# A 16-head attention layer's start is re-ordered: parts of q and k made per half from PSUM, all q/k projections before the row maxima, value projections between them, gates computed during the input load

## The reference

```python
x = x + _L0_attn_a_ref(_layernorm(x), Wq, bq, Wk, bk, Wv, bv, Wo, bo, gates...)   # layer "aa"
x = x + _L0_ffn_ref(...); x = x + _L0_attn_b_ref(...); x = x + _L0_ffn_ref(...)
x = x + _L1_attn_a_ref(_layernorm(x), Wqkv, Wproj, bproj)                         # layer "ac"
x = x + _L1_ffn_ref(...); x = x + _L1_attn_b_ref(...); x = x + _L1_ffn_ref(...)
...
q, k, v = (proj(Wq, bq), proj(Wk, bk), proj(Wv, bv))
scores = jnp.einsum('bhqd,bhkd->bhqk', q, k) / math.sqrt(hd)
order_bonus = jax.nn.sigmoid(order_gate) * (position_bias * 0.05)
justice_adjustment = jax.nn.sigmoid(justice_gate) * ((mean_score - scores) * 0.1)
attn = jax.nn.softmax(scores + order_bonus + justice_adjustment + ..., axis=-1)
out = jnp.einsum('bhqk,bhkd->bhqd', attn, v)
return out @ Wo.T + bo
```

## Time and profile before

| what | value |
|---|---|
| median of 3 runs | 1435.81 us (1435.34 to 1439.43) |
| profiled execution, span from the first to the last instruction | 1435.6 us |
| TensorE matmul busy | 1349.0 us (94%) |
| VectorE busy | 895.4 us (62%) |
| ScalarE busy | 694.1 us (48%) |
| GpSimd busy | 278.4 us (19%) |
| input load | 0 to 14.6 us |
| layer aa, before the first row maximum / the 14 slots | 14.6 to 37.9 us / 37.9 to 58.7 us |
| layer ac, before the first row maximum / the 14 slots | 626.5 to 641.9 us / 641.9 to 662.6 us |

### The profile page before, as it was taken

The page is one execution under the profiler, slowest core; times in us unless marked ns, Lnnn a source line. Parts: engine busy times, 40 slices in busy tenths (PEclk is TensorE's granted clock), DMA queues, the critical chain, the costliest instruction groups (busy, mean ns, idle before and its releaser), DMA issues. The chain is left out here.

```text
span 1435.6 us, 32894 instructions
## 1 busy us (share of the span) xinstructions
PE 1349.0 (94%) x13699; PEld 738.4 (51%) x13707; DVE 895.4 (62%) x2147; ACT 694.1 (48%) x1037; POOL 278.4 (19%) x343
## 2 busy tenths in 40 slices
PE   7999998999679988999999989999899999989999
PEld 3355555474345774563555554436355555555436
DVE  3899994666486456749999826433655555535431
ACT  5487776646483325535777752111444444442110
POOL 4322513001230000043000000110533433210110
PEclk9999999999879999999999999999999999999999
DMA  3323300100300000022222030000300000000000
GB/s 87 70 38 65 65 14 1 34 1 2 118 0 4 17 1 16 0 45 42 43 39 36 3 117 0 1 0 7 64 13 17 15 13 14 9 1 1 1 0 29
DMA packets 33957, 37.47 MB, mean 26 GB/s; under 512 B 9153, under 2 KB 24626, under 8 KB 33810
## 3 DMA queue, kind: packets, MB, share of 16 engines
q1 hardware_dynamic: 33810, 35.39, 11.2%
HBM read 18.43 MB, written 1.07 MB: 14 GB/s over the span
## 5 line engine op out<-in xcount | busy, mean ns | idle before, releaser
L616 DVE TENSOR_REDUCE row_max_pieces<-psum 128x1 f32<-128x512 f32 (+3 forms) x672 | 406.9, 647 | 112.4 <-PE psum L510 109.7
L717 ACT ACTIVATE probs<-psum 128x1024 f32<-128x1024 f32 (+7 forms) x384 | 343.7, 900 | 212.6 <-PE psum L510 212.2
L564 PE MATMUL psum<-probs,v_ones 128*32 128x256 f32 (+1 forms) x2688 | 238.8, 376 | 9.0 <-POOL probs L499 4.6
L510 PE MATMUL psum<-q_all,k_head 97*32 97x512 f32 (+3 forms) x1536 | 190.7, 487 | 0.0
L510 PE MATMUL psum<-k_stack,q_stack 96*32 96x512 bf16 x2048 | 158.8, 379 | 3.5 <-DMA k_stack<-arena 1.3
L510 PE MATMUL psum<-q_stack,k_stack 97*32 97x512 bf16 x2048 | 157.8, 379 | 0.0
L564 PEld LDWEIGHTS psum<-probs,v_ones 128*32 128x32 f32 x2688 | 88.0, 109 | 85.1 <-POOL probs L499 21.6
L510 PE MATMUL psum<-k_head_bf,q_all_bf 80*32 80x512 bf16 (+3 forms) x768 | 93.0, 328 | 2.3 <-ACT k_head_bf L2487 1.1
L510 PEld LDWEIGHTS psum<-q_all,k_head 97*32 97x32 f32 x1536 | 78.8, 109 | 29.5 <-issue 3.9
L510 PEld LDWEIGHTS psum<-k_stack,q_stack 96*32 96x32 bf16 x2048 | 56.5, 95 | 72.1 <-DVE row_max_pieces L616 20.4
L510 PEld LDWEIGHTS psum<-q_stack,k_stack 97*32 97x32 bf16 x2048 | 58.3, 96 | 49.4 <-ACT probs L717 3.7
(11 more groups left out here) (368 smaller groups left out, 2085.6 us busy)
## 6 DMA issues: line engine op xcount, KB each, us to landing
q_stack<-arena SPq DMA_DIRECT2D x32, 96.0 KB, 2.7
k_stack<-arena SPq DMA_DIRECT2D x32, 96.0 KB, 2.6
arena<-gd_g_sums SPq DMA_DIRECT2D x6, 512.0 KB, 6.1
q_stack<-arena SPq DMA_DIRECT2D x32, 64.0 KB, 2.3
k_stack<-arena SPq DMA_DIRECT2D x32, 64.0 KB, 2.3
x_tokens<-in_x SPq DMA_DIRECT2D x4, 256.0 KB, 3.6
k_stack<-arena SPq DMA_DIRECT2D x32, 32.0 KB, 2.3
q_stack<-arena SPq DMA_DIRECT2D x32, 32.0 KB, 2.0
```

The lines of the kernel that those rows point to most:

```text
L510: last = pe.matmul(o[j:j + 32], by[:, j:j + 32], rows, **flags)
L564: last = pe.matmul(psum[32 * g:32 * g + VW, PVB, a - g * D:D], V[:, c, h, :], pr[:, n % PB, a:(g + 1) * D], start=(c == 0), stop=(c == (2 ...
L616: last = dve.reduce_max(mx[:, h % 2, qt, i:i + 1], o[:, 0:plain], AX.X)
L717: act.activation(pr[:, n % PB, q_from(c):], psum[:, 2 * (n % 2):2 * (n % 2) + 2, :].rearrange("p a n -> p (a n)")[:, q_from(c):], ACT.Exp, ...
```

## The change

- The gates, the positions and the biases of q, k and v come in three DMAs that ScalarE issues at the start of `load_inputs`. ScalarE and VectorE compute gates, key factor and score scale before their part of the norm there; the sigmoid is made from an exponential, an addition and a reciprocal. A square root of a constant follows on ScalarE, before the first one of the norm. At the end of the load VectorE scales Wq by the score scale.
- All 16 projection matmuls of q and k come first, the second features' into banks 4 to 7. The first three pieces of the ring wait until ScalarE has taken these (`pe_ring`).
- Of the first features each half (512 tokens) is a unit of its own: ScalarE makes the high part straight from PSUM (L886), VectorE the rest from PSUM, bias and high part in one operation (L935), ScalarE the middle (L890), VectorE the low part (L938). The second features go over `qk_full` as before.
- The 16 value matmuls (now without the bias matmul) stand in slots 0 to 12: two each in slots 1, 3 and 5, one each in the others; they write banks 0 to 3. The copies of the values stand among the parts of the second features on ScalarE. The filler matmuls are gone. Before the first key scores TensorE waits for all eight copies.
- v's bias is added in `project_out`, when the attended features are copied (`Copy` becomes `Identity` with a bias).

```diff
 def load_inputs(nc, core, x_dram, loads, gates, wq, wq_loaded):
...
             def _(dve):
+                gates.dve(dve)
                 for t in range(NT):
                     dve.wait_ge(x_loaded[t // 2], 16)
                     norm.dve(dve, t)
+                gates.scale_queries(dve, wq, wq_loaded)
...
             def _(act):
+                gates.loads(act)
+                gates.act(act)
                 act.wait_ge(made, 4)
+                act.activation(spare[:], core.eps[:], ACT.Sqrt)
                 norm.act(act)
...
+    def act(self, act):
+
+        act.wait_ge(self.loaded, 48)
+        act.activation(self.g[:], self.g[:], ACT.Exp, scale=-1.0).then_inc(self.squashed, 1)
+        act.wait_ge(self.steps, 3)
+        act.activation(self.factor[:], self.factor[:], ACT.Exp).then_inc(self.exp_done, 1)
+
+    def dve(self, dve):
+
+        g, esc = self.g, self.score_scale
+        dve.wait_ge(self.squashed, 1)
+        dve.tensor_scalar(g[:], g[:], 1.0, None, ALU.add).then_inc(self.steps, 1)
+        dve.wait_ge(self.steps, 1)
+        dve.reciprocal(g[:], g[:]).then_inc(self.steps, 1)
+        dve.wait_ge(self.steps, 2)
+        dve.tensor_scalar(self.factor[:], self.pos, g[:, 1:2], 0.05, ALU.mult, ALU.mult).then_inc(self.steps, 1)
+        dve.tensor_scalar(esc[:], g[:, 0:1], -0.1 / HD ** 0.5, 1.0 / HD ** 0.5, ALU.mult, ALU.add).then_inc(self.steps, 1)
+        dve.wait_ge(self.steps, 4)
+        dve.tensor_scalar(self.bqk[:, 0, :], self.bqk[:, 0, :], esc[:, 0:1], None, ALU.mult)
...
+            V_BETWEEN = {m: (1, 2)[m in (1, 3, 5)] for m in range(13)}
+            V_UP_TO = {m: sum(V_BETWEEN[i] for i in range(m)) for m in range(14)}
...
                 def pe(pe):
                     pe.wait_ge(first_loaded, 32)
+                    for n in range(4):
+                        u = ORDER[n]
+                        for half in range(NH2):
+                            for k in range(KT):
+                                last = pe.matmul(Prep.bank(n, half), (wq, wk)[u // 2][:, k, (u % 2) * P:(u % 2 + 1) * P],
+                                                 XNT[:, k, cols(half)], start=(k == 0), stop=(k == KT - 1))
+                            last.then_inc(qk_ready, 1)
+                    pe.wait_ge(loaded, 48)
+
+                @staticmethod
+                def pe_ring(pe, n):
+                    pe.wait_ge(full_done, n + 1)
+
+                @staticmethod
+                def pe_between(pe, m):
+                    if m == 0:
+                        pe.wait_ge(r1, FIRST)
+                    for i in range(V_UP_TO.get(m, 0), V_UP_TO.get(m + 1, 0)):
+                        t, k = i // KT, i % KT
+                        last = pe.matmul(psum[:, t // 2, (t % 2) * D:(t % 2 + 1) * D], XNT[:, k, t * P:(t + 1) * P],
+                                         wv[:, k, :], start=(k == 0), stop=(k == KT - 1))
...
+                    def high_of(n, half):
+                        act.wait_ge(qk_ready, NH2 * n + half + 1)
+                        act.activation(parts[:, ORDER[n], 0, cols(half)], Prep.bank(n, half), **copied(n)).then_inc(hi, 1)
+
+                    def middle_of(n, half):
+                        act.wait_ge(r1, NH2 * n + half + 1)
+                        act.activation(parts[:, ORDER[n], 1, cols(half)], rest[:, n, cols(half)], ACT.Copy).then_inc(mid, 1)
...
                     for n in range(2):
                         for half in range(NH2):
-                            keep_full(n, half)
-                        high(n)
-                    middle(0)
-                    middle(1)
-                    for t in range(NT):
-                        keep_v(t)
+                            high_of(n, half)
+                            middle_of(n, half)
                     for n in range(2, 4):
                         for half in range(NH2):
                             keep_full(n, half)
+                    for n in range(2, 4):
                         high(n)
+                        for t in range(2 * (n - 2), 2 * (n - 1)):
+                            keep_v(t)
                         middle(n)
+                    for t in range(4, NT):
+                        keep_v(t)
...
                 def dve(dve):
+                            dve.wait_ge(hi, j + 1)
...
+                            dve.scalar_tensor_tensor(rest[:, n, cols(half)], Prep.bank(n, half), by,
+                                                     parts[:, ORDER[n], 0, cols(half)], op, ALU.subtract).then_inc(r1, 1)
+                            dve.wait_ge(mid, j + 1)
+                            dve.tensor_tensor(parts[:, ORDER[n], 2, cols(half)], rest[:, n, cols(half)],
+                                              parts[:, ORDER[n], 1, cols(half)], ALU.subtract).then_inc(lo, 1)
```

More of the change, by code:

```diff
@@ L158, in pe_behind, with load_inputs @@
             self.keep_busy(pe, 0, 1)
-def load_inputs(nc, core, x_dram, loads):
+def load_inputs(nc, core, x_dram, loads, gates, wq, wq_loaded):
     X, ident = core.X, core.ident
@@ L167, in load_inputs @@
         norm = Norm(core, "in", tmp)
+        spare = core.sb("spare_root", [P, 1], F32, tmp)
         with nc.Block() as block:
@@ new lines, in attention16 @@
+            cols = lambda half: slice(half * HALF, (half + 1) * HALF)
+            parts_done = lambda n: NH2 * (n + 1) if n < 2 else FIRST + n - 1
+            scale_of = lambda n: HD ** -0.5 if gates is None and ORDER[n] // 2 == 0 else 1.0
+            bias_of = lambda n: gates.bqk[:, ORDER[n] // 2, ORDER[n] % 2:ORDER[n] % 2 + 1]
+            V_BETWEEN = {m: (1, 2)[m in (1, 3, 5)] for m in range(13)}
+            V_UP_TO = {m: sum(V_BETWEEN[i] for i in range(m)) for m in range(14)}
+            def loads(sp):
@@ L812, in pe @@
                     pe.wait_ge(loaded, 48)
-                    if gates is not None:
-                        pe.wait_ge(gates_loaded, 80)
-                    for t in range(NT):
-                        o = psum[:, 4 + t // 2, (t % 2) * D:(t % 2 + 1) * D]
-                        for k in range(KT):
-                            last = pe.matmul(o, XNT[:, k, t * P:(t + 1) * P], wv[:, k, :],
-                                             start=(k == 0), stop=(k == KT - 1 and gates is None))
-                        if gates is not None:
-                            last = pe.matmul(o, core.ones[:], bv[:], start=False, stop=True)
-                        last.then_inc(v_ready, 1)
@@ L845, in keep_full @@
-                        scale = HD ** -0.5 if gates is None else esc[:]
-                        act.activation(full[:, n % 2, half * HALF:(half + 1) * HALF],
-                                       psum[:, 2 * (n % 2) + half, :], ACT.Identity,
-                                       bias=bqk[:, which, f:f + 1] if gates is not None else 0.0,
-                                       scale=1.0 if which else scale).then_inc(full_done, 1)
+                        act.activation(full[:, n % 2, cols(half)], Prep.bank(n, half), **copied(n)).then_inc(full_done, 1)
@@ L983, in attention16, with project_out @@
                             exp_kw={}, shift_dt=BF16, head_loads=Stacks, prep=Prep, aside=aside)
-        project_out(nc, core, tag, O, wo, next_loads)
-def project_out(nc, core, tag, O, wo, next_loads, tiles=KT, OT=None, xn=None):
+        project_out(nc, core, tag, O, wo, next_loads, bias=gates.bv if gates else None)
+def project_out(nc, core, tag, O, wo, next_loads, tiles=KT, OT=None, xn=None, bias=None):
     X, psum, ident = core.X, core.psum, core.ident
@@ L1024, in _ @@
                     act.wait_ge(turned, n + 1)
-                    act.activation(OT[:, f, half * HALF:(half + 1) * HALF], psum[:, n % 4, :],
-                                   ACT.Copy).then_inc(kept, 1)
+                    act.activation(OT[:, f, half * HALF:(half + 1) * HALF], psum[:, n % 4, :], ACT.Identity,
+                                   bias=0.0 if bias is None else bias[:, f:f + 1]).then_inc(kept, 1)
                 norm.act(act)
@@ L2468, in pe_last, with pe_ring @@
                 @staticmethod
+                def pe_ring(pe, n):
+                    pass
+                @staticmethod
                 def pe_last(pe):
@@ L2692, in build @@
         first = attention16_early(core.sem, core, "aa", a["a_wq"], a["a_wk"])
[L2693 removed]
+        gates = Gates(core, {"justice": a["a_justice"], "order": a["a_order"], "rows": a["a_rows"]})
+        load_inputs(nc, core, a["x"], first[-1], gates, first[0], first[2])
         ternary_scope = ExitStack()
         ternary = Ternary(core, (a["f_up"], a["f_gate"], a["f_down"]), ternary_scope)
[L2696 to L2697 removed]
+        attention16(nc, core, "aa", first, a["a_wv"], a["a_wo"], a["a_bo"], gates, None, ternary)
         core.layer_done()
```

146 lines of the change are left out of this document (58 added, 88 removed).

## The result

| | median, us | runs | ratio to before, 95% interval |
|---|---|---|---|
| before | 1436.01 (1435.34 to 1439.43) | 4 | |
| changed kernel | 1426.64 (1423.93 to 1428.59) | 4 | 0.9921 (0.9896 to 0.9946) |
| forecast | 1424.5 (1421.5 to 1430.5) | | 0.992 |

In all tables one execution is left out: a later kernel ("both mended") once took 2308 us at a granted clock of 0.55.

A forecast was written before the change was run, and what follows sets the result against it. Steady loop full on TensorE and VectorE and left alone; gains at the starts of aa and ac: -6.1 - 2.2 - 0.9 - 2.2 + 0.1 = -11.3 us, from 1435.8 to 1424.5 us, range 1421.5 to 1430.5.

The forecast's parts named there:

- What bounds the kernel: Steady loop full on TensorE and VectorE, left alone; value projections bound aa's start, parts and DMA ac's, TensorE the slots.
- The load: Input load before aa: gates land at 4.7, first square root at 7.3, so the load gets 1.1 us longer.
- the upper bound: Input load: gate DMAs land at most 5.1 us after issue, making the load 3.2 us longer.
- the root later than 8: Input load: sign that the gates forecast is wrong; the first square root was forecast near 7.3.
- the gates land late: Rival, input load: gate DMAs land 5.1 us after issue, VectorE waits; 2.1 us more, 1426.6 us in all; chance 0.20.
- the table's drain: Input load: the skill's extra 1.38 us per table switch, about 2.66 in all; load 2.5 us longer, total 1425.9.
- the lower bound: Input load: gate DMAs land 1.8 us after the last one's issue, making the load 0.2 us longer.
- aa up to the first scores: Start of layer aa: parts are the bound, unit period 2.12 us; first scores at 31.8 against 37.91, 6.1 less.
- The slots: 14 slots before the first key scores, aa and ac: VectorE bounds eleven; 18.1 instead of 20.3 us, 2.2 less each.
- Slots stay bound by TensorE: Rival, slots of aa and ac: they take up to 1.6 us each as before; 1428.9 us in all; chance 0.12.
- project_out: Four copies get a bias pointer, 0.67 for 0.60, one or two on the path: 0.1 us more.
- the rival that ends slower: TensorE's clock falls in the slots without fillers: 2.34 or 3.2 us a slot, 1458.8 us in all; chance 0.05.

The follow-up runs named there:

- both mended: Changed kernel with one DMA for the gates, VectorE's gates behind its norm, key factor's exponential at layer aa's start: median 1424.18 us, ratio to before 0.9913.
- short last unit: Changed kernel with k's second features projected by one matmul per half instead of two: 1436.68 us in one run, slots of aa 21.43 us.

## Why the prediction was right or wrong

**What bounds the kernel** held. In aa the value projections had been the bound, in the slots TensorE; what started earlier was carried to the end of each layer, with 0.3 us on top in the loop that I did not forecast and have not explained.

**The load**: the term was mis-sized, 1.1 for a measured 3.8. The step that failed is "I take 3.0, which is what x's first DMA took": the landing took 5.7, which is also beyond the 5.1 that I took for the upper bound, and the root later than 8 was my own sign of being wrong. The rest of the chain was right: 2.54 us from the exponential's start at 7.48 to the first root at 10.02, with 2.6 forecast. So the rival "the gates land late" is what happened, with +2.7 for a forecast +2.1. Its reason was only half right. The gates did not just wait in a queue: their three DMAs, two of them in 4-byte pieces, also slowed x's, whose median landing went from 3.6 to 6.1 us. One DMA of the same data brought the gates' landing down to 2.4. As to the table's drain, the trace disagrees with what the Trainium skill, "ScalarE: Activation LUTs", What ACT_TABLE_LOAD costs, counts: 1.29 us from the table load's start to the next activation, and 1.31 us from the end of the activation before (8.59 to 9.90), where by the page a switch takes 2.66. Two numbers of the working were off as well and changed little. With a landing of 1.8 us my own chain puts the root at 6.1, so the lower bound was 0.1 us less than before and not 0.2 more, and the range's lower end 1421.3. And VectorE ended its norm 2.4 us before the block's end (12.26 of 14.63), not 1.5; the scaling of Wq hid either way.

**aa up to the first scores**: -7.06 for a forecast -7.2 (without the load). The bound was the parts and the DMAs, as said (the short last unit shows it), though TensorE's projections end at 34.5, only 0.15 before the scores. The unit's period was 2.05 instead of 2.12, since ScalarE's high part of the next half starts 0.1 before the middle part has ended. In aa that is 0.2 us in three periods, and it was used up: the first half unit was ready 3.8 us after the first projection instead of 3.5. In ac the three periods (1.88, 1.99 and 1.99) are 0.5 us shorter together, which is more than the 0.37 us by which ac did better (-1.27 for -0.9).

**The slots**: -2.47 and -2.64 for -2.2. VectorE waits 0.30 for each pair with a double slot, three times: 0.9 where I took 0.17 each and 0.5 in all, so the ring smooths nothing. But its maxima take 0.62 us back to back, not the 0.647 of the profile's page, whose group mixes four forms. The two misses cancel for the most part, which is luck. "Slots stay bound by TensorE" did not happen; where all of eight slots are double, they follow each 1.61 us, so a slot's price of 1.60 was right.

**project_out**: 17.84 before, 17.82 after: the bias costs nothing.

**The sum**: -11.3 forecast; -10.2 measured by stages. That it is so near is partly luck: the load alone missed by 2.7 us, and the slots (0.7), the start of ac (0.4) and the two loops (0.6), where I had forecast nothing, gave 1.7 back. That the median (1426.64) is the late gates' 1426.6 is luck for the same reason. The medians give -9.4, the profiled executions -13.4. What lies between is not of the change: the recurrent layer and both feed-forward layers, whose code is the same, differ by 2.7 us between the two profiles, and what follows ac by 0.5.

**The clock**: the rival that ends slower did not occur in the changed kernel, whose slots run at 1.00; in ac TensorE is busy 17.59 of their 18.10 us by the profile, not the 90% that I had counted. But its mechanism lies near. Where slots held row-maximum scores alone, the clock fell to 0.50 in both layers of both kernels that have such slots, and in the short last unit it fell in aa's slots and cost 3.2 us. So "TensorE no longer has fillers" named the right danger, and the value matmuls may be what averts it. At the lower clock a slot with one value matmul took 2.12 us (38.66 to 40.78 in the short last unit), priced at 2.34; where VectorE bounds the slots, as with scores alone, the lower clock cost less, some 0.8 us.

## What to carry to other kernels

Work moved into an "idle" early stage stands in each engine's queue: ask what its first wait waits for, and put it behind what must not be late. Replicate a scalar in the array's layout rather than by a DMA of 4-byte pieces beside large loads. Fill slots that another engine bounds with the small pieces of work that stood ahead of them; such work may also be what keeps TensorE's clock up, so read the granted clock of the slots before it is taken out. When a price is tested, price both kernels by it, and look for the wait itself and not only for the total.

## What the runs showed of the hardware

- Three small DMAs (two of them 128 pieces of 4 bytes) issued beside four of 256 KB went with a transfer rate of 140, 85 and 144 GB/s in the microseconds from 3 to 6, against 329, 281 and 303 in the kernel before, and x's median landing went from 3.6 to 6.1 us. With one DMA of 64 bytes per partition it was 3.5 us. Size and number of the DMAs' pieces were not varied apart.
- With row-maximum scores alone, 0.40 us of matmuls in each 0.60, TensorE's granted clock fell from 1.00 to 0.50, four times of four (two kernels, two layers), and came back in the steady loop.
- The same code takes different times with the clock that TensorE is granted. The two rows are the changed kernel in its first and in its repeated profile, the start of the first routed layer; its stretch up to the next layer's loads took 146.8 and 153.5 us:

```profile
840.00:860.00 20.00, 18.20 (x85) 11.09 (x85) 9.30 (x64) 4.54 (x8) 0.38 (x1) 1.00 0.06 16
```
```profile
840.00:860.00 20.00, 18.14 (x54) 10.94 (x53) 4.48 (x39) 3.19 (x6) 0.38 (x1) 0.66 0.12 30
```

The program is the same, and the gap before the layer's first matmul was 1.26 us in both, but TensorE's clock just before was not: in project_out it was lower in the first profile and full in the repeat.

```profile
820.00:830.00 10.00, 8.17 (x68) 6.08 (x61) 1.42 (x6) 5.96 (x9) 0.00 (x0) 0.83 0.31 85
```
```profile
820.00:830.00 10.00, 8.17 (x110) 4.70 (x105) 1.09 (x6) 6.72 (x10) 0.00 (x0) 1.00 0.08 19
```

Over all 14 profiles the routed stretch has two values, 146.8 to 146.9 us in eight and 153.5 to 153.6 in six, and so has the project_out ahead of it, 17.8 to 17.9 us in five and 16.3 in nine. In each of them the long value goes with a granted clock below 1.00 in that stretch, and no profile has the long value in both. The recurrent layer with the feed-forward layer behind it, from norm_weight's load to the next weights' load, took 225.8 to 233.3 us. Why the clock is granted in one execution and not in another is open. These differences, 6.7, 1.5 and 7.5 us, make single times of this kernel worth little below 10 us; stages from timelines agree within 0.1 to 0.2 us where the clock is the same, but for the load, whose first projection came at 18.30 to 19.25 us in three profiles of the changed kernel.
